# Solving inside the state chain of a gated delta-rule kernel, padded 128x128 products, and a new order of work

## What is computed

```python
def step(S, inp):
    qt, kt, vt, gt, bt = inp
    S = S * gt[..., None]
    pred = jnp.einsum('bhk,bhkv->bhv', kt, S)
    delta = (vt - pred) * bt[..., None]
    S = S + kt[..., None] * delta[:, :, None, :]
    o = jnp.einsum('bhk,bhkv->bhv', qt, S)
    return (S, o)
```

## Time and profile before

| | |
|---|---|
| median of 3 runs | 2520.49 us |
| lowest and highest run | 2516.51 and 2522.57 us |
| span of the profiled execution | 2516.3 us (the only time given for it; the fastest run is 0.2 us above) |
| TensorE busy | 2261.4 us, 90% |
| VectorE busy | 1972.7 us, 78% |
| ScalarE busy | 1721.0 us, 68% |
| GpSimd busy | 1264.2 us, 50% |

### The profile page before, as it was taken

How to read it: one execution, slowest core, us unless ns; L and a number is a source line. 1 busy time by engine, 2 the same in 40 slices (tenths; PEclk the granted TensorE clock), 3 DMA queues, 4 the chain that set the end, 5 groups by cost and what they waited for, 6 DMA issues and landing times.

```text
span 2516.3 us, 87483 instructions
## 1 busy us (share of the span) xinstructions
PE 2261.4 (90%) x38320; PEld 1331.3 (53%) x38320; DVE 1972.7 (78%) x3031; ACT 1721.0 (68%) x3490; POOL 1264.2 (50%) x1004
## 2 busy tenths in 40 slices
PE   6689999999999999999999999998768877888777
PEld 3456666666666666666665666666423322323223
DVE  3768888888888887877887878887358789898981
ACT  2667788778887787777776778786655757656532
POOL 0445554555455444544443445553045587867960
PEclk8899999999999999999999999999879999999889
DMA  1000000000000000000000000001063062534400
GB/s 59 23 10 14 14 14 24 13 14 14 19 19 13 13 14 24 20 20 20 20 20 19 20 20 24 14 6 28 22 176 67 31 142 56 118 67 101 101 30 9
DMA packets 49837, 91.10 MB, mean 36 GB/s; under 512 B 7980, under 2 KB 17964, under 8 KB 48944
## 3 DMA queue, kind: packets, MB, share of 16 engines
q1 hardware_dynamic: 49456, 85.50, 13.1%
HBM read 74.71 MB, written 10.76 MB: 34 GB/s over the span
## 4 chain that ended last, share of the span: by engine, by line
PE 53%; DVE 19%; ACT 11%; issue 9%; POOL 6%; DMA 1%; SPq 1%; POOLq 0%; DVEq 0%; ACTq 0%
PE bank L396 9%; PE bank L500 5%; PE pair L623 4%; DVE cv L708 4%; PE bank L467 4%; PE bank L657 3%; PE pair L611 3%; POOL dBu L2289 3%; PE bank L593 2%; DVE bank L1921 2%; PE bank L436 2%; ACT Y L1084 2%; DVE kq L796 2%; PE bank L616 2%; PE pair L1587 2%
## 5 line engine op out<-in xcount | busy, mean ns | idle before, releaser
L708 DVE SCALAR_TENSOR_TENSOR cv<-raw,taps,cv 128x1024 f32<-128x1024 f32 x288 | 395.0, 1372 | 20.0 <-ACT cv L972 18.2
L396 PE MATMUL bank<-xn,W 128*128 128x512 f32 x768 | 370.7, 613 | 0.0
L1245 POOL TENSOR_TENSOR R<-kq,gate 128x1024 f32<-128x1024 f32 x32 | 77.6, 2424 | 494.2 <-ACT gate L1038 494.2
L2289 POOL TENSOR_TENSOR dBu<-dtu_wide,Bn 128x1024 f32<-128x1024 f32 x128 | 301.9, 2375 | 45.8 <-DVE bank L1921 26.5
L1268 POOL TENSOR_TENSOR kq<-kq,tot 128x512 f32<-128x512 f32 x128 | 220.2, 1720 | 206.4 <-PE bank L467 206.4
L2175 ACT ACTIVATE bank<-dt_wide,m_A 128x512 f32<-128x512 f32 x256 | 172.5, 687 | 109.5 <-DVE hc L1929 72.3
L396 PEld LDWEIGHTS bank<-xn,W 128*128 128x128 f32 x768 | 135.6, 193 | 120.7 <-issue 112.2
L971 ACT ACTIVATE raw<-bank 128x512 f32<-128x512 f32 x192 | 114.9, 598 | 94.6 <-PE bank L396 91.9
L1270 POOL TENSOR_TENSOR R<-R,tot 128x512 f32<-128x512 f32 x128 | 164.4, 1284 | 0.0
L623 PE MATMUL pair<-vT,kT 64*128 64x128 f32 x1024 | 126.3, 323 | 28.6 <-DVE vT L885 28.6
L467 PE MATMUL bank<-R,kq 128*32 128x64 f32 (+1 forms) x10240 | 134.0, 204 | 15.3 <-POOL R L1270 8.1
(11 more groups left out here) (305 smaller groups left out, 5677.3 us busy)
## 6 DMA issues: line engine op xcount, KB each, us to landing
dt_wide<-ssm_wide SPq DMA_DIRECT2D x60, 256.0 KB, 4.9
dtu_wide<-ssm_wide SPq DMA_DIRECT2D x60, 256.0 KB, 7.9
W<-in_head_w SPq DMA_DIRECT2D x32, 448.0 KB, 3.6
WO<-in_out_w SPq DMA_DIRECT2D x32, 192.0 KB, 2.4
ssm_wide<-hfa SPq DMA_DIRECT2D x8, 512.0 KB, 2.8
ssm_wide<-vc SPq DMA_DIRECT2D x8, 512.0 KB, 2.9
Bn<-ssm_rows SPq DMA_DIRECT2D x64, 64.0 KB, 5.3
Cn<-ssm_rows SPq DMA_DIRECT2D x64, 64.0 KB, 4.2
```

The source lines that it names most:

```text
L396: m = pe.matmul(psum[bank][:, :], w[:, (kind * KT + k) * P:(kind * KT + k + 1) * P], xn[:, k, b, cols], start=k == 0, stop=k == KT - 1)
L708: dve.scalar_tensor_tensor(cv[m % 2][:, :, :], raw[m % 2][:, :, i:i + SEG], taps[:, h, KQV[n], i:i + 1], cv[m % 2][:, :, :], MUL, ADD).the ...
L2289: pool.tensor_tensor(dBu[at % AHEAD][:, :, :], dtu_wide[n % 2][:, half * DT2:(half + 1) * DT2, :], spread(Bn[sg][:, :], 1, DT2), MUL).then ...
```

## The change

U and W are gone, and so is the turning of the decayed keys. The chain of a chunk is now pred = kR S (L567), v - pred on VectorE, the solve Y (v - pred) as one 128x128 matmul (L582) on a block-diagonal Yd, a copy of the result from PSUM by ScalarE (L1089), and the outer product (L588). The turned keys lie in kTd, one 128-row tile a batch with zeros in the other batch's rows, so the outer product uses the whole array. The products within a chunk (L595) use the whole array too, on a block-diagonal ATd. The zeros are written once by GpSimd at the start, in place of three smaller memsets on VectorE. There is one gate buffer in place of two, two vT in place of three, one kTd in place of two kT; knorm has two. A tile tg takes the turned output and the tanh. PLACES and EARLY_AT hold other numbers; FRONT_AT and FFN_AT are the old ones, rounded.

```diff
 PLACES = [
-    (-1, [62.44, 98.25, 98.25, 107.3, 135.23, 144.87]),
-    (0, [8.7, 38.71, 40.58, 49.64, 55.51, 60.66]),
-    (0, [46.77, 46.77, 61.32, 64.82, 65.54, 66.08]),
-    (0, [65.56, 71.92, 71.92, 72.19, 84.93]),
...
+    (-1, [59.08, 104.17, 121.84, 123.58, 133.11, 142.5]),
+    (0, [14.29, 36.12, 37.56, 45.5, 51.34, 58.67]),
+    (0, [42.59, 47.25, 60.1, 65.98, 69.26, 102.7]),
+    (0, [75.99, 76.17, 78.48, 78.62, 88.12]),
...
@@ TensorE: turn_k, solved @@
-                for q in range(2):
-                    bank = take()
-                    if q == 0:
-                        pe.wait_ge(*up_k.at(g, NL))
-                    for c in range(4 * q, 4 * q + 4):
-                        m = pe.transpose(psum[bank][:, (c % 4) * P:(c % 4 + 1) * P],
-                                         R[s][:, 0, c, :, :].rearrange("p b t -> p (b t)"), eye[:, :])
...
-            def solved(g):
...
-                            m = pe.matmul(psum[bank][rows_of(b), (c % 4) * P:(c % 4 + 1) * P],
-                                          Y64[rows_of(b), c, :, :].rearrange("p h i -> p (h i)"), vT[g % 3][rows_of(b), c, :])
...
-                        m = pe.matmul(psum[w_banks[b]][:, c * CH:(c + 1) * CH], kRT(g)[rows_of(b), c, :],
-                                      Y64[rows_of(b), c, :, :].rearrange("p h i -> p (h i)"))
@@ TensorE: state @@
                         pe.wait_ge(*s_set.at(g, c - 1))
                     else:
-                        pe.wait_ge(*wT_set.at(g, 1))
-                        if g == 0:
+                        pe.wait_ge(*up_k.at(g, NL))
+                        if g:
+                            pe.wait_ge(*s_set.at(g - 1, NC - 1))
+                        else:
                             pe.wait_ge(*s_zeroed.at(0))
                     for b in range(NB):
-                        m = pe.matmul(psum[CHAIN[0]][rows_of(b), 0:P], WT[s][:, c, rows_of(b)], src[:, b, :])
+                        m = pe.matmul(pred[rows_of(b), :], R[s][:, 0, c, b, :], src[:, b, :])
                     m.then_inc(pred_full.sem)
-                    if c == 4:
+                    if c == 0:
+                        pe.wait_ge(*up_q.at(g))
+                        if g:
+                            pe.wait_ge(*og_set.at(g - 1, 1))
+                    elif c == 4:
                         pe.wait_ge(*og_set.at(g, 0))
                     for b in range(NB):
                         pe.matmul(psum[OUT][rows_of(b), (c % 4) * P:(c % 4 + 1) * P], R[s][:, 1, c, b, :], src[:, b, :],
                                   start=c % 4 == 0, stop=False, skip_group_check=True)
                     yield
                     pe.wait_ge(*d_set.at(g, c))
+                    if c == 0:
+                        pe.wait_ge(*off_kept.at(g))
+                    pe.matmul(solved, Yd[s][:, c, :], vT[s][:, c, :]).then_inc(delta_full.sem)
+                    yield
+                    pe.wait_ge(*delta_set.at(g, c))
                     if c % 4 == 0:
                         pe.wait_ge(*kT_set.at(g, c // 4))
                     for b in range(NB):
-                        m = pe.matmul(psum[CHAIN[b]][:, P:2 * P], kT[s][rows_of(b), c, :], vT[g % 3][rows_of(b), c, :])
+                        m = pe.matmul(outer[:, b, :], kTd[:, b, c, :], vT[s][:, c, :])
                     m.then_inc(outer_full.sem)
                     yield
                     if c % 4 == 3:
                         if c == 3:
                             pe.wait_ge(*at_set.at(g, 1))
                         for c4 in range(c - 3, c + 1):
-                            for b in range(NB):
-                                m = pe.matmul(psum[OUT][rows_of(b), (c4 % 4) * P:(c4 % 4 + 1) * P],
-                                              AT[s][rows_of(b), c4, :], vT[g % 3][rows_of(b), c4, :], start=False,
-                                              stop=True, skip_group_check=True)
+                            m = pe.matmul(psum[OUT][:, (c4 % 4) * P:(c4 % 4 + 1) * P], ATd[s][:, c4, :],
+                                          vT[s][:, c4, :], start=False, stop=True, skip_group_check=True)
@@ ScalarE: inverse, turn_k, solved, out_gate, state @@
-                for q in range(2):
-                    bank = turn.next()
-                    act.wait_ge(*kR_turned.at(g, q))
...
                     act.wait_ge(*k_turned.at(g, q))
-                    if q == 0 and g >= 2:
-                        act.wait_ge(*outer_full.at(g - 2, NC - 1))
-                    act.activation(kT[g % 2][:, 4 * q:4 * q + 4, :].rearrange("p c d -> p (c d)"), psum[bank][:, :],
-                                   ACT.Copy).then_inc(kT_set.sem)
+                    if g:
+                        act.wait_ge(*outer_full.at(g - 1, 4 * q + 3))
+                    elif q == 0:
+                        act.wait_ge(*blocks_zeroed.at(0))
+                    for b in range(NB):
+                        m = act.activation(kTd[rows_of(b), b, 4 * q:4 * q + 4, :].rearrange("p c d -> p (c d)"),
+                                           psum[bank][rows_of(b), :], ACT.Copy)
+                    m.then_inc(kT_set.sem)
...
             def state(g):
-                for _ in range(2 * NC + 1):
-                    yield
+                for c in range(NC):
+                    yield
+                    act.wait_ge(*delta_full.at(g, c))
+                    act.activation(vT[g % 2][:, c, :], solved, ACT.Copy).then_inc(delta_set.sem)
+                    yield
+                    yield
+                    if c == 3:
+                        yield
@@ GpSimd @@
+            for t in ATd + Yd:
+                pool.memset(t[:, :, :], 0.0)
+            pool.memset(kTd[:, :, :, :], 0.0).then_inc(blocks_zeroed.sem)
```

More of the change, by code:

```diff
@@ L263, in hybrid_block @@
         view = psum[PROD][:, :].rearrange("p (c a i) -> p c a i", c=NC, a=2)
-        outer = pair[:, :].rearrange("p (b n) -> p b n", b=NB)[:, :, P:2 * P]
-        def kRT(g):
-            return flat(gate[g % 2]).rearrange("p (c d) -> p c d", d=P)
-        def th(g):
-            return R[g % 2][:, 0, :, :, :].rearrange("p c b t -> p (c b t)").rearrange("p (c v) -> p c v", v=P)
+        pred, solved, outer = (psum[CHAIN[0]][:, 0:P], psum[CHAIN[0]][:, P:2 * P],
+                               psum[CHAIN[1]][:, 0:NB * P].rearrange("p (b n) -> p b n", b=NB))
         class Turn:
@@ L851, in turn_k @@
             def turn_k(g):
-                for q in range(2):
-                    turn.next()
-                    yield
                 turn.next()
                 yield
-                turn.next()
-            def solved(g):
-                turn.next()
-                yield
-                turn.next()
-                yield
-                turn.next()
                 turn.next()
@@ L930, in att_vector @@
             att_drive((first_vector(dve, turn), front_vector(dve, turn)(0)), conv(0), conv(1), conv(2), dots, gating, turn_v, products, inverse, turn_k,
-                      solved, out_gate, state, output)
+                      out_gate, state, output)
         def att_scalar(act):
@@ L1037, in gating @@
                 act.wait_ge(*gate_lin.at(g))
-                act.activation(flat(gate[s]), flat(gate[s]), ACT.Exp, scale=neg_a[:, h:h + 1]).then_inc(gate_set.sem)
+                act.activation(flat(gate), flat(gate), ACT.Exp, scale=neg_a[:, h:h + 1]).then_inc(gate_set.sem)
             def turn_v(g):
@@ L1088, in inverse @@
                 for w in (1, 3):
[L1089 removed]
+                    m = act.activation(BZ[quad(w), :, :], inv[quad(w), 1, :, :], ACT.Copy, scale=-1.0)
                 m.then_inc(z_kept.sem)
@@ L1293, in turn_k @@
             def turn_k(g):
-                for _ in range(3):
-                    yield
-            def solved(g):
-                for _ in range(2):
-                    yield
+                yield
             def out_gate(g):
@@ L1304, in state @@
             def state(g):
-                for _ in range(2 * NC + 1):
+                for _ in range(3 * NC + 1):
                     yield
```

175 lines of the change are left out of this document (50 added, 125 removed), and 67 rows, old and new, of tables (EARLY_AT, FFN_AT, FRONT_AT, PLACES).

## The result

| | before | changed | ratio, 95% interval |
|---|---|---|---|
| median of the runs | 2520.13 us (2516.51 to 2522.57) | 2611.69 us (2607.93 to 2617.67) | 1.0368 [1.0351, 1.0385] |
| profiled span | 2516.3 us | 2613.0 us | |
| mean granted clock | 0.967 | 0.948 | |
| attention loop, 31 periods | 1647.7 us | 1741.6 us | |
| before the first, behind the last | 159.4 and 709.2 us | 153.2 and 718.1 us | |

The change costs 92 us by the medians. The spans differ by 96.7 us: 93.9 of them in the 31 periods (3.0 a head), 6.2 gained ahead of them, 9.0 lost behind them. A period runs from one scaling of WO on ScalarE to the next.

What follows compares the result with a forecast made beforehand. TensorE's issue bounds the attention loop; 47.7 us of work plus 5.0 of waiting for ScalarE, adjusted, made 52.9 a head against 50.6. 2516.3 + 71 - 5 - 1 + 5 = 2586, median 2590 us; own range 2511 to 2700, with rival 2 2500 to 2690.

Steps and rivals of the forecast that it cites:

- TensorE's saving: TensorE's work per head: 4.8 us removed, solves and wider outer product added, products within a chunk cheaper; net -2.9 us.
- The outer product in the full shape: State update on TensorE: two matmuls take 0.45 instead of 0.42 us, +0.2 a head; the skill's tiling rule would add 3.4.
- Seven loads a head: ScalarE's activation tables: seven loads instead of three, blamed on the moved silu of v; four more at 1.30, 5.2 us.
- Rival 4: ScalarE's table loads: each costs 2.7 us with its drain, +170 us on top, 2760 us; chance 0.01.
- TensorE stands 5.0 us at chunk 0: Chunk 6's copy to next chunk 0's outer product: ScalarE needs 21.4 us, TensorE 16.4, so TensorE waits 5.0 each head.
- the column of ScalarE: ScalarE's instructions added up from chunk 6's copy until the next head's chunk 0 outer product can start: 21.4 us.
- Everything else hidden: Other moves: fewer gate, key and v buffers cost 0; DVE and POOL keep their work; DMA issues don't move.
- rival 2: TensorE's granted clock falls after the waits; two slowed groups a head cost 1.8 us, +56 us, 2646 us; chance 0.12.
- the transposes behind the late copy: TensorE's L611 waits for the output norm's scaled rows, which come behind the late copy: about 0.5 us a head.
- ScalarE has 10.8 us of slack a head: ScalarE in the kernel before: busy 39.8 of 50.6 us a head, the rest read as slack.
- rival 1: ScalarE's queue does not bite, loads fall into idle gaps; only TensorE's saving of 90 us is left, 2430 us; chance 0.12.
- The start and the end: Outside the loop: three memsets fewer on DVE, -1 us; a hop of some 0.7 us in eight uncovered chunks, +5 us.

Runs made afterwards that it cites:

- e10: From e5, the silu of the values placed behind the output norm's Ln and Exp, ahead of the key copies and chunk 0's copy, two loads a head: 2524.4 us.
- e2: The changed kernel with one more table load a head, behind the gate's last Exp, inside the stretch between the copies of chunks 6 and 0: 2651.1 us.
- e7: The kernel before with four more table loads a head, none of them in the state chain: 2621.8 us.
- e1: The changed kernel, order untouched, with activation tables asked for only where needed, four loads a head instead of seven: 2558.6 us.
- e9: From e5, the silu of the values moved behind chunk 0's copy, two table loads a head instead of four: 2567.9 us.
- e11: From e5, the silu of the values moved behind chunk 2's copy, along with the queries' first projection, two loads a head: 2530.4 us.
- e12: From e11, the first half of the turned keys ahead of chunk 0's state, and the output norm's Ln and Exp behind chunk 0's copy: 2570.8 us.
- e5: From e1, two places of the dots moved so that the small matmuls of L404 and L407 stand apart: 2542.8 us.
- e6: The changed kernel with two places of the dots moved so that the small matmuls of L404 and L407 stand apart, seven loads a head: 2658.7 us.
- e8: From e1, the silu of the values moved behind chunk 0's copy, two table loads a head instead of four: 2583.1 us.
- e3: The changed kernel with one more table load in 25 of 32 heads, behind the scaling of WO, outside the stretch: 2623.8 us.
- e4: The changed kernel with the copy of the solved rows done by VectorE instead of ScalarE: 2711.1 us.

## Why the prediction was right, point by point

The time (2590 forecast, 2611.7 measured), its sign and its range held. A head came to 53.6 us where the steps gave 52.9.

- **TensorE's saving, -2.9 a head (bounds -3.1 to -1.9).** Measured -2.5 in busy time, from e10, which issues the same matmuls at full clock. But the terms that the prediction named come to -1.8 there, just outside its bounds (from start to start, over 13 heads, stops taken out): the removed groups -4.8 as forecast, the solves 2.3 instead of 2.0, the products within the chunks -0.2, and the outer product as said next. The other -0.7 came from groups that the sum left alone, such as the output's transposes (1.24 to 0.96 us a head), its last product (3.71 to 3.42) and the projections (11.07 to 10.87). That the total is so near is luck in part.
- **The outer product in the full shape, +0.2.** This term was too small. In the kernel before it takes 0.42 us in each of 104 chunks. In e10 it takes 0.53 on average, from 0.44 to 0.64 by what follows it: 0.9 us a head more. The doubled step that the tiling rule would give (3.4) is not there, but "the two row halves gain nothing from being separate" doesn't hold either: they save a fifth.
- **Seven loads a head, 1.30 each.** Seven groups, 31 or 32 each, 1283 ns; the next instruction starts 1.29 after (347.17 to 348.46). e2 confirms the price: 1.23 us for a load in the stretch. Rival 4, a drain on top, is out.
- **Why there are seven.** The count and the places were right, the reason in part not. The moved silu of v explains three loads (its own, and those of the output norm's Ln and Exp) less one (the tanh, which had one in 31 heads and now finds its table there). The two before the gate's Exp and Ln are not its doing: in PLACES the gate's Exp moved from 83.72 to 71.73 and the preload of `dots` from 72.19 to 78.62, so the pair now stands ahead of that preload, behind the silus of keys and queries (the last one at 329.16 us, no load until L981's at 335.26). With the silu of v back in its place those two loads would still be there.
- **TensorE stands 5.0 us at chunk 0.** Right in place, cause and order (first the solve for Yd, then the outer product for the copy), too large: 1.0 and 2.4 us in this head, 3.5 together as the mean of 13. From the solve of chunk 6 (334.16) to the outer product (355.93) it is 21.8 us, where the column of ScalarE gave 21.4. TensorE is idle for 4.5 of them (0.49, 0.59, 1.03 and 2.38 us) and so works for 17.3, at full clock, where its column gave 16.4. So the columns were short by 0.4 and 0.9 us, and 1.1 of the remaining stall lie in the stop in L407 and the wait for UM, ahead of the last two waits.
- **Everything else hidden.** The sum missed two terms: the stops in dense groups (1.2 us a head), of which the 13 heads of before show 0.8 us in all, and the clock. TensorE is busy for 48.3 us a head at a granted clock of 0.97, for 46.9 at 1.00 in e10; the 1.4 us between them are put down to the clock, which fits the 44.3 us at half clock (22 us lost, at most 1.7 a head). That is rival 2's mechanism at three quarters of its price (1.8), beside the forecast's stall and not in place of it. Measured, a head is 46.9 of work, 1.4 of clock, 3.5 of ScalarE's waits, 1.2 of stops, 0.4 for UM and 0.2 of small ones: 53.6.
- **Luck.** Against these 3.2 us that it had at nothing (clock, stops, UM, small ones), the sum had 2.7 too much: 1.5 in the stall, 0.4 of the 0.5 for the transposes behind the late copy (L611 waits 1.4 us in 13 heads), and the 0.8 of waits that it carried over from before. The period of 52.9 is within 0.7 of the measured one because these nearly cancel.
- **"ScalarE has 10.8 us of slack a head", and rival 1 on the strength of it.** The sum did not use it, but the reading was wrong. e7 puts four loads (5.1 us) into the kernel before and pays 3.2 us a head. Idle time in one half of a head is no room in the other.
- **The start and the end.** -6.2 and +9.0 instead of -1 and +5, both outside the loop.

The reading of the cause was right and incomplete. Taking three loads out of the stretch gives back 53 us of the 92 (e1), and two table changes with three moved places bring the changed kernel level with the one before (e10). That the change would win with a better order is not shown: four kernels were expected at or below it (e1, e9, e11, e12) and none got there; each kept or met another wait, behind ScalarE, at the output's transposes or for VectorE, and in e9 and e12 most of the loss is clock.

## What to carry to other kernels

Before you count idle time of an engine as slack, look where in the period it lies and add up the queue between two instructions that the bounding engine waits for; a load that changes activation tables cost nearly its full 1.3 us there and about 0.5 in the one quieter place tried. When steps move in the order, list the table that each activation around them needs: here a silu that moved behind the preload of `dots`, and a gate's Exp that moved ahead of it, turned three loads a head into seven, and no line of the diff says so. And when every queue is nearly full, taking away one wait mostly shows the next: read after each edit which instruction waits now, and look at the granted clock: here one stop of 2.6 us a head (e9) cost more than two of about 1.0 (e5), since the clock went with it.

## What the runs showed of the hardware

- **TensorE stops in the middle of a group where nothing is to be waited for.** Timeline of the changed kernel:

```profile
548.38 0.59 PE L407 MATMUL bank<-kq 128*32 128x32 f32 x43
550.62 0.39 PE L407 MATMUL bank<-kq 128*32 128x32 f32 x21 [1.65 <-issue]
...
552.86 3.19 PE L620 MATMUL bank<-tg,WO 128*128 128x512 f32 x4
```

  43 of the 64 matmuls (counted in the profile's records), 1.65 us of nothing, the other 21; then L620 at 3.19 us, where the same four take 1.88 in e9: the mean granted clock in these 3.19 us is 0.59. The changed kernel has 29 such stops over 0.5 us, 35.3 us in all, 27 of them in L404, L407 or L487; the kernel before has none over 0.5 us, and they come where those groups stand in a row. Where two stops are in one head, they lie 127 or 128 matmuls apart; from head to head it is mostly 1011 or 1012, or 1137 to 1142: about eight or nine times 126.5. Each of these matmuls has a weight load of its own. The profile's list of queues has one for instructions, with packets of 16 KB:

```profile
q8 instruction: 285, 4.67, 0.7%
```

  The Trainium skill (Runtime: NRT & Kernel Launch, Instruction fetch mechanics) says that instructions come in 16 KiB blocks of 256 and that crossing a block is mostly hidden. 128 matmuls with 128 weight loads are 256, which agrees with the distance of the stops; that crossing is hidden does not hold in these dense runs. The packets agree with it too: the trace has 72,032 matmuls and weight loads of TensorE and 285 packets, and 285 times 256 is 72,960 (before: 76,640 and 303 packets, 77,568). And the packets' times tell what the stops are. In every one of the 29 stops TensorE goes on 1.24 to 1.54 us after a packet of this queue has ended and 2.19 to 2.76 us after it began; of moments picked at random one in twenty lies that far behind a packet's end. It is the same in the 39 stops of e1 (1.22 to 1.57 us). In the dense groups 128 matmuls take 1.6 to 2.0 us (from start to start 64 of L487 take 1.03, of L404 0.91, of L407 0.7), which is less than the 2.19 us and more from a packet's beginning to the going on. All of this says that TensorE waits for its instructions there. No run took these waits away by themselves, and what they cost is not isolated: e5, with most of them gone, gained 16 us, and in e6 the gain was drowned.
- **The clock after a stop.** The longest stop that comes in every head, and the granted clock over the 13 heads: 2.6 us and 0.96 (e8, e9), 2.4 and 0.95 to 0.97 (changed kernel, e2, e3, e6), 2.2 and 0.97 (e4), 1.9 and 0.96 (e12), 1.6 and 1.00 (e10), 1.4 and 0.99 (e11), 1.1 and 0.99 (e1, e5). The kernel before waits for 1.0 us a head in two pieces, none over 1.1, and has 1.00.
